# One base row on GpSimd, first weights loaded a stage ahead, and identity products on TensorE in a macaron block (mixture of experts, attention, mixture of experts)

## The reference

```python
x = x + 0.5 * ffn(layernorm(x), w_router, w_gate, w_up, w_down)
x = x + attn(layernorm(x), Wq, bq, Wk, bk, Wv, bv, Wo, bo)     # 16 heads of 32, RoPE, softmax
x = x + 0.5 * ffn(layernorm(x), w_router, w_gate, w_up, w_down)

# ffn: xt is [8192, 512], 32 experts, capacity C = 320 rows per expert
logits = xt @ w_router
top1 = argmax(softmax(logits)); gate = the probability of top1
pos = cumsum(onehot(top1))[t, top1] - 1; accepted = pos < C
slot = top1 * C + pos                       # rows over the capacity are dropped
y = (silu(buf @ w_gate) * (buf @ w_up)) @ w_down   # per expert
return xt + where(accepted, y[slot] * gate, 0)
```

## Time and profile before

| | |
|---|---|
| median of three runs | 4290.29 us |
| the profiled execution's own time | 4291.16 us |
| its span in the trace | 4289.4 us |
| mean granted TensorE clock | 0.962 of 2.4 GHz |
| PE, PEld, DVE, ACT, POOL busy | 94%, 61%, 69%, 49%, 57% |
| r1 | 0 to 212 us |
| e1 | 212 to 970 us |
| qkv | 970 to 1577 us |
| attention | 1577 to 3239 us |
| r2 | 3239 to 3532 us |
| e2 | 3532 us to the end |

### The profile page before, as it was taken

The page is one execution under the profiler, slowest core; times in us unless marked ns, Lnnn a source line. Parts: engine busy times, 40 slices in busy tenths (PEclk is TensorE's granted clock), DMA queues, the critical chain, the costliest instruction groups (busy, mean ns, idle before and its releaser), DMA issues. The chain is left out here.

```text
span 4289.4 us, 68901 instructions
## 1 busy us (share of the span) xinstructions
PE 4027.0 (94%) x24768; PEld 2627.7 (61%) x24768; DVE 2957.0 (69%) x3993; ACT 2106.5 (49%) x3591; POOL 2434.7 (57%) x1500
## 2 busy tenths in 40 slices
PE   5489999998999979999999999999996969999999
PEld 3379899886888853333333333333335758998998
DVE  5567777766666667777777777777744866777776
ACT  5433333332222217777777777777772434333332
POOL 2334334324555647888888888888881333443442
PEclk7589999998999989999999999999998989999999
DMA  6265555535555555656665666656636845555552
GB/s 220 99 213 197 171 184 194 175 120 185 182 175 182 177 150 131 134 132 137 139 141 130 135 138 143 134 130 137 140 87 224 290 156 203 196 188 174 187 193 105
DMA packets 493061, 700.29 MB, mean 163 GB/s; under 512 B 217684, under 2 KB 220008, under 8 KB 492752
## 3 DMA queue, kind: packets, MB, share of 16 engines
q1 hardware_dynamic: 459984, 629.09, 52.0%
q0 software_dynamic: 30720, 66.62, 4.1%
q10 hardware_dynamic: 2048, 0.53, 0.1%
HBM read 518.55 MB, written 194.54 MB: 166 GB/s over the span
## 5 line engine op out<-in xcount | busy, mean ns | idle before, releaser
L1858 DVE TENSOR_REDUCE kept_big<-att_mx 128x2 f32<-128x2048 f32 x496 | 1137.5, 2293 | 436.4 <-PE att_mx L1892 436.1
L1802 ACT ACTIVATE att_p<-att_st 128x512 f32<-128x512 f32 x2048 | 1086.8, 602 | 412.6 <-PE att_st L1915 350.8
L1762 POOL TENSOR_TENSOR att_pairsum<-att_p,att_p 128x1024 f32<-128x1024 f32 x512 | 1207.2, 2383 | 87.8 <-ACT att_p L1802 74.1
L944 ACT ACTIVATE e_sg<-e_gp 128x320 f32<-128x320 f32 x256 | 112.1, 438 | 732.7 <-PE e_up L208 684.1
L925 DVE TENSOR_TENSOR e_w<-e_raw,e_w 128x2048 fp32r<-128x2048 f32 x192 | 439.1, 2287 | 41.9 <-ACT e_w L920 40.8
L1915 PE MATMUL att_st<-att_q,att_k 128*128 128x512 f32 x1344 | 452.6, 438 | 0.2 <-ACT att_p L1802 0.2
L1915 PEld LDWEIGHTS att_st<-att_q,att_k 128*128 128x128 f32 x1344 | 216.1, 187 | 327.2 <-ACT att_p L1802 220.0
L920 ACT ACTIVATE e_w<-e_raw 128x2048 fp32r<-128x2048 f32 x192 | 367.0, 1911 | 53.1 <-DMA e_raw<-in_w_gate 49.1
L1925 PE MATMUL att_st<-att_p,att_v 128*32 128x512 f32 x2688 | 349.3, 603 | 0.0
L389 POOL DMA_INDIRECT table<-r_pay,r_slot_i x128 | 143.4, 1121 | 354.8 <-DVE r_pay L577 320.7
L894 POOL DMA_INDIRECT x<-e_xg,e_meta x64 | 102.3, 1599 | 410.4 <-DVE e_xg L987 388.4
(11 more groups left out here) (177 smaller groups left out, 8262.2 us busy)
## 6 DMA issues: line engine op xcount, KB each, us to landing
e_raw<-in_w_gate SPq DMA_DIRECT2D x64, 1024.0 KB
e_raw<-in_w_up SPq DMA_DIRECT2D x64, 1024.0 KB
e_raw<-in_w_down SPq DMA_DIRECT2D x64, 1024.0 KB
r_ao<-ao SPq DMA_DIRECT2D x32, 1024.0 KB
att_q<-q SPq DMA_DIRECT2D x126, 256.0 KB, 5.3
att_k<-k SPq DMA_DIRECT2D x126, 256.0 KB, 7.4
kept_w<-q SPq DMA_DIRECT2D x110, 256.0 KB, 4.7
kept_w<-k SPq DMA_DIRECT2D x66, 256.0 KB, 7.3
```

Of the source, the lines that this page charges most:

```text
L1762: nc.gpsimd.tensor_tensor(out=pairsum[h][g][:, :], in0=pr[h][2 * g][:, :], in1=pr[h][2 * g + 1][:, :], op=ALU.add).then_inc(s_add, 1)
L1802: nc.scalar.activation(pr[h][kt][:, half(c)], st[u % NB], ACT.Exp, scale=SCALE).then_inc(s_exp, 1)
L1858: nc.vector.tensor_reduce(out=big[p % 2][:, :, qt], in_=mx[:, :, :, :].rearrange("p h c k -> p h (c k)"), axis=AX.X, op=ALU.max).then_inc( ...
```

## The change

It has three parts.

First, in r1 alone, the base row of the last tile of each group (j = 3) is made by POOL instead of ACT, with a multiply and an add by the same two vectors. ACT makes three (`OURS`). The waits on `s_base` count three, and a new semaphore `s_side` counts POOL's.

Second, weights go a stage ahead. Two tiles of 1 MB are kept over two stages. In a routing stage SP loads gate and up of expert 0 into them when group 13's base has been stored; in e1, behind the last expert's loads, SP loads wq and wv into the same two tiles once expert 30's weights are split. In qkv ACT makes the high parts of wq and wv before the first `norm`, and DVE the low part of wq before it measures the first group.

Third, `keep_busy` gives PE plain float32 products of the 128x128 identity with itself, whose result nobody reads. In r1 three of them stand in front of every turn from group 1 on and of every `products` from group 2 on; 36 stand at the end of r1 and r2, 28 at the start of e1 and e2, 20 at the start of qkv, 40 at the end of attention.

```diff
+def keep_busy(nc, out, ident, n):
+    for _ in range(n):
+        nc.tensor.matmul(out[:, 0:P], ident[:, :], ident[:, :], start=True, stop=True)
 # route, sync
             def store_base(r):
-                sp.wait_ge(s_base, TJ * (r + 1))
+                sp.wait_ge(s_base, OURS * (r + 1))
+                if not attn:
+                    sp.wait_ge(s_side, r + 1)
...
                 store_base(r)
+                if r == NG - 3:
+                    for tile, src, landed in first:
+                        sp.dma_start(tile[:, :, :], src).then_inc(landed, 16)
 # route, gpsimd
+            def last_base(r):
+                j = TJ - 1
+                pool.wait_ge(s_lin, 2 * (r + 1))
+                pool.wait_ge(s_base_stored[r % 2], 16 * (r // 2))
+                nc.gpsimd.tensor_scalar(base[r % 2][:, j, :], x[r % NX][:, j, :], grow[r % 2][:, j:j + 1],
+                                        shift[r % 2][:, j:j + 1], ALU.mult, ALU.add).then_inc(s_side, 1)
...
             for w in range(NR):
+                if not attn and w + 1 < NR:
+                    last_base(2 * w + 2)
                 pool.wait_ge(s_slots, w + 1)
                 for j in range(TR):
+                    if not attn and w + 1 < NR and j == TR // 2:
+                        last_base(2 * w + 3)
                     nc.gpsimd.indirect_dma_start(
 # route, scalar (three places)
-                        bases(r, range(TJ))
+                        bases(r, range(OURS))
 # route, tensor
                     if r < NG:
                         for j in range(TJ):
+                            keep_busy(nc, spare, ident, 3)
                             turn(r, j)
                     positions(w)
                     if r < NG:
+                        keep_busy(nc, spare, ident, 3)
                         products(r)
                         for j in range(TJ):
+                            keep_busy(nc, spare, ident, 3)
                             turn(r + 1, j)
+                        keep_busy(nc, spare, ident, 3)
                         products(r + 1)
...
+            keep_busy(nc, spare, ident, 36)
 # experts
             load_meta(0, 0)
-            load_raw(0, 0, (0,))
             sp.dma_start(ident[:, :], cst["ident"]).then_inc(s_const, 16)
-            load_raw(0, 0, (1,))
...
+            for w, (src, landed) in enumerate(after):
+                sp.wait_ge(s_hi, 3 * (E - 2) + w + 1)
+                sp.wait_ge(s_lo, 3 * (E - 2) + w + 1)
+                sp.dma_start(raw[w][0][:, :, :], src).then_inc(landed, 16)
...
+            keep_busy(nc, yp[0], ident, 28)
             for m in range(KH):
                 turn(0, 0, m)
 # qkv, scalar
+            hi_w(ORDER[0])
+            hi_w(ORDER[1])
             norm(0, 0)
-            hi_w(ORDER[0])
 # qkv, vector
+            lo_w(ORDER[0])
             measure(0, 0, (0, 1))
             measure(0, 0, (2, 3))
             normalise(0, 0)
-            lo_w(ORDER[0])
+            lo_w(ORDER[1])
 # qkv, tensor
+            keep_busy(nc, pps[:, 0, :], ident, 20)
 # attention, tensor, at its end
+            keep_busy(nc, mx[:, 0, 0, :], ident, 40)
```

More of the change, by code:

```diff
@@ L223, in route @@
     NA = 3
+    OURS = TJ if attn else TJ - 1
     with S.ctx:
@@ L467, in _ @@
                     if r < NG:
-                        bases(r + 1, range(TJ))
+                        bases(r + 1, range(OURS))
         @block.vector
@@ L739, in _, with experts @@
                         back(r + 1)
-def experts(nc, name, moved, rows, table, wg, wu, wd, cst):
+            keep_busy(nc, spare, ident, 36)
+def experts(nc, name, moved, rows, table, wg, wu, wd, cst, first, after=()):
     S = Space(nc, name)
@@ L755, in experts @@
         side = sb("side", [P, 1])
-        raw = [S.pair(sb, f"raw{w}", [P, KD, F]) for w in range(3)]
+        raw = [[tile, sb(f"raw{w}", [P, KD, F])] for w, (tile, _, _) in enumerate(first)]
+        raw.append(S.pair(sb, "raw2", [P, KD, F]))
         split = [[S.pair(sb, f"w{w}_{par}", [P, KD, F], F32R) for par in range(2)] for w in range(3)]
@@ L915, in hi_weight @@
             e, par = number(i, b), b % 2
-            act.wait_ge(s_raw[w][par], 16 * (turns(i, b) + 1))
+            if w < 2 and par == 0:
+                act.wait_ge(first[w][2], 16)
+                act.wait_ge(s_raw[w][par], 16 * turns(i, b))
+            else:
+                act.wait_ge(s_raw[w][par], 16 * (turns(i, b) + 1))
             act.wait_ge(s_gu, past(KF * (e - 1)))
@@ L1108, in _, with qkv @@
             rounds_out(DEPTH, E, step)
-def qkv(nc, name, x_in, wT, bias, cst, q_out, k_out, v_out, kept):
+def qkv(nc, name, x_in, wT, bias, cst, q_out, k_out, v_out, early_w, kept):
     S = Space(nc, name)
@@ L1127, in qkv @@
         w = [S.pair(sb, f"w{m}", [P, KD, D], F32R) for m in range(3)]
-        area = [sb(f"area{m}", [P, 4, GROUP]) for m in range(3)]
+        area = [early_w[m][0] if m in early_w else sb(f"area{m}", [P, KD, D]) for m in range(3)]
         wraw = area
@@ L1990, in macaron, with early @@
              for n, many in (("r1", 2), ("e1", 8), ("r2", 2), ("e2", 8))}
-    route(nc, "r1", moved["r1"], x, w_router, cst, x1, table[0])
-    experts(nc, "e1", moved["e1"], x1, table[0], w_gate, w_up, w_down, cst)
-    with Kept(nc) as kept:
-        qkv(nc, "qkv", x1, (wq, wk, wv), (bq, bk, bv), cst, q, k, v, kept)
-        attention(nc, "att", q.rearrange("s b d q -> s (b d) q"), k.rearrange("s b d q -> s (b d) q"),
-                  v.rearrange("b g t c -> (b g) t c"), cst, ao.rearrange("s b d q -> s (b d) q"), sums, inverse, kept)
-    route(nc, "r2", moved["r2"], x1, w_router, cst, out, table[1], attn=(ao, wo, bo))
-    experts(nc, "e2", moved["e2"], out, table[1], w_gate, w_up, w_down, cst)
+    def early(kept, name):
+        tiles_of = [kept.enter_context(nc.sbuf_tensor(f"{name}_first{w}", [P, KD, F], F32)) for w in range(2)]
+        return [(tile, src[0:1, :, :].rearrange("o (k p) f -> p (o k) f", p=P),
+                 nc.alloc_semaphore(name=f"{name}_first_in{w}"))
+                for w, (tile, src) in enumerate(zip(tiles_of, (w_gate, w_up)))]
+    with ExitStack() as kept:
+        first = early(kept, "e1")
+        landed = [nc.alloc_semaphore(name=f"w_landed{m}") for m in range(2)]
+        after = [(src.rearrange("(k p) n -> p k n", p=P), sem) for src, sem in zip((wq, wv), landed)]
+        early_w = {m: (first[w][0], landed[w]) for w, m in enumerate((0, 2))}
+        route(nc, "r1", moved["r1"], x, w_router, cst, x1, table[0], first)
+        experts(nc, "e1", moved["e1"], x1, table[0], w_gate, w_up, w_down, cst, first, after)
+        with Kept(nc) as held:
+            qkv(nc, "qkv", x1, (wq, wk, wv), (bq, bk, bv), cst, q, k, v, early_w, held)
+            attention(nc, "att", q.rearrange("s b d q -> s (b d) q"), k.rearrange("s b d q -> s (b d) q"),
+                      v.rearrange("b g t c -> (b g) t c"), cst, ao.rearrange("s b d q -> s (b d) q"), sums, inverse, held)
+    with ExitStack() as kept:
+        first = early(kept, "e2")
+        route(nc, "r2", moved["r2"], x1, w_router, cst, out, table[1], first, attn=(ao, wo, bo))
+        experts(nc, "e2", moved["e2"], out, table[1], w_gate, w_up, w_down, cst, first)
 def constants(np):
```

32 lines of the change are left out of this document (22 added, 10 removed).

## The result

The changed kernel takes 4276.4 us (median of 7 runs) where the kernel before takes 4290.3, a ratio of 0.9968 with the interval 0.9958 to 0.9977. The profiled execution took 4276.7 us with a span of 4274.9, 14.5 less than before. By the first instruction of each stage, r1 gave 11.0 of them (e1 begins at 201.4 in place of 212.4), e1 1.3, qkv 0.8, e2 1.7, and attention with r2 took back 0.3.

The account below looks back on a forecast made before the run. PE is nearly full elsewhere; only r1, a chain with no engine full, and the seams, some 350 of 4289 us, were reachable. Terms -16 (r1), -9 (e1, e2), -1 (qkv), 0 gave -26: 4264 us, range 4243 to 4286.

Parts of the forecast that it names:

- Part 1: r1, base row on POOL at 1.2 us: -0.7 us a round in the second half, up to +1.2 in the first.
- rival (a): r1: held-back events vanish as turns come earlier in the scatters; rounds of 17.5 us, 4244 us in all; chance 0.16.
- Part 2: r1, identity products: clock up for most of r1, both products 1.08 us; rounds of 20.7 us, r1's term -16 us.
- the second half's sum: r1, second half of a round: base row 0.7, products 1.7 and last turns 0.2 make it 2.6 us shorter.
- the 0 for the first half: r1, first half of a round: scatters' +1.2 against faster positions and shorter ACT; 0 us, between -3 and +1.3.
- rival (b): Only the seams pay: scatters set r1's first half, DVE's chain eats the rest; r1 0, sum -10, 4280 us; chance 0.12.
- Part 3: e1 and e2: gather 2.9 us sooner, gate and up at full clock; some -4.5 us each, -9 for both.
- qkv: Start of qkv: projecting begins later, at 990.6, but at full clock; -1 us in all, bounds +2.3 and -3.
- Attention to r2: Seam into r2: 0 us, as PE still waits for a DMA after 40 products and nothing warms it.
- Rival (c): r1: clock stays at half, rounds of 28 us; +33 less 10 at the seams, 4313 us; chance 0.06.
- rival (d): Seams: gather late by its own latency, cold products delay turns; e1, e2 +1.5 each, qkv +2; 4279 us; chance 0.08.

Follow-up runs that it names:

- best: Changed kernel with products only in r1's second halves and e1/e2 starts (seven more there), second base row behind the scatters, qkv's low parts earlier: 4265.7 us, 0.9951 of before.
- base_act: Changed kernel with all four base rows on ACT again, all identity products kept: 4289.8 us, 1.0006 of the kernel before.
- no_products: Changed kernel without any identity product; weights ahead and the base row on GpSimd stay: 4267.2 us, 0.9955 of the kernel before.
- no_seam: Changed kernel with the threes in r1's rounds but without the 36, 28, 20 and 40 products at stage ends and starts: 4275.3 us, 0.9972 of before.
- late_again: Changed kernel with identity products only in the second half of r1's rounds, none at the seams, on chip D: 4267.8 us, 0.9956 of before.
- after_again: The changed kernel, unchanged, run again on chip D: 4274.7 us, 0.9972 of the kernel before.
- orders_np: Changed kernel without products, DVE's low parts moved ahead at the starts of e1, e2 and qkv: 4236.6 us, 0.9974 of before on chip C.

## Why the prediction was right or wrong

The time was in the range and on the right side, at half the forecast's gain (14.5 of 26 us). Every stage gave less than its term: r1 11.0 for 16, e1 and e2 3.0 for 9, qkv 0.8 for 1. And in r1 even the sign of a term was wrong: one part gave far more than its price and the other took instead of giving. That their sum came to 11 of 16, and the time into the range, is luck.

**Part 1** put the base row on GpSimd at -0.7 us a round, and at up to +1.2 in the first half. The price was too high (0.78 us, not 1.2), and its effect was mis-sized most: -2.3 a round and -16.0 in r1 on chip B. I had counted ACT's time in the second half only. ACT is free earlier in the first half too, and the turns' events come 4.5 us earlier; that they come before the scatters hold anything back is the likely reason, not shown by itself. The next event is still late, so 1.1 us a round is left of it. That is rival (a)'s mechanism, in part. It came with the base row and, it seems, not by the pause: best, on D and with products in the second half, has no pause, and its turns come through as early. On C, where nothing is held back, the weights and the base row together are worth only 3 us.

**Part 2** had the second half's sum: 13.8 to 11.4 us is -2.4 for -2.6, at PEclk 0.85. But it had it by luck. I let both products fall to 1.08 us; the first ones stayed at 1.86 to 1.94 in four of the six rounds, as PE stands before them, and 0.6 came from where I had nothing, the second products' event, no longer late.

The step that failed is the 0 for the first half. Up to the products it measured +1.1 (copies at 9.9 for 8.9 us), inside my bound, and the 1.2 of the base row, rival (b), isn't the whole of it: base_act has no base row among the scatters, and its last copies come 10.9 us after choose. What the term should have been is read from the last scatter. On A, B and D ACT's copy behind the first products starts after the end of the last scatter in 58 of 60 rounds; on C, with eight scatters, it starts 1.4 to 5.1 us before that end in all 18. So where events are late the scatters close the first half, and a faster PE only brings choose nearer to them. In the changed kernel the last scatter ends 10.4 us after choose and that copy follows 2.1 us later; in no_products these are 9.5 and 0.9. Of the 2.1 us in all, 0.9 is choose coming earlier against the scatters and 1.2 is PE's work coming later behind them.

The net is a median 8.0 us longer with the threes, from no_products to no_seam on B; the threes of the first half alone cost 6.8 from late_again to after_again on D, with the small part of the seams in it. On C the clock that the products raise is worth 14 us.

The Trainium skill (TensorE: Matmul & The Clock Gate, Part 4) says that transposes don't count as busy time of PE in the same way. With 0.59 without products and 0.85 with them the runs on B and A agree; on C orders_np rose to 0.76 with no product, so transposes and routing products alone don't always leave it at half.

**Part 3.** The gather came 1.9 us sooner, not 2.9. The clock at the first turn is full, as forecast, but it fell behind PE's 2.33 us between the turns, and gate and up ran at half: the 2.4 of the matmuls' clock were not gained. That made -1.3 and -1.7 of -4.5 each. no_seam and no_products show that the 28 products gave nothing that the stages' times can tell: what is left is the weights. best, with seven products in that place, keeps the clock at 1.0, but of the 2.4 a stage no more than 1.3 shows in its stages' times, for a reason that stays open.

**qkv** was -0.8 for -1, projecting later than before as forecast (19.5 us after the begin, 20.5 forecast). That it came near is two errors again: projecting began 1.0 us sooner than forecast, and its first 5.7 us ran at half the clock where I had it full. That the low part ahead of the statistics could not use the time before was a choice of the kernel and no necessity: the wait for the identity can stand behind it.

**Attention to r2** gave nothing, as said; r2's first matmul is at half the clock. Rival (c) is wrong, the clock rose; rival (d) is wrong in the gather and in the turns. Rival (b), only the seams pay, is wrong too: r1 gave 11.0. But its ground, a first half closed by the scatters, is what the runs bear out.

**Open.** What holds PE's events, and in best its issue, during the scatters on A, B and D and not on C. The traces show that it isn't the scatters alone, since C has them too, nor anything in the kernel, since one kernel ran both ways. That more instructions on PE make it worse is shown in part, by the 1.2 us above. Whether it belongs to a chip or to the time of a run can't be told, as each chip was used at one time only. How the number of scatters bears on it was not tested where events are late.

## What to carry to other kernels

Filling an engine's gaps to keep its clock up can cost more than it gives where other work depends on its events being prompt. Price each part of a change with a run of its own: the whole (0.9968) hid that it is 0.9955 without the products. Measure a wait from the event that ends it, here the last scatter, and not from the start of the round, which moves when something else gets faster. A clock gained at a seam is kept only if the gaps behind it are filled too, down to the first dense matmuls. And a gain that hangs on late events is to be measured on more than one chip before it is believed. Stage times are of one execution; look how far it lies from its kernel's median before reading a few us out of them.

## What was unexpected of the hardware

One kernel took 4287.5 us on one chip and 4248.7 on another, with no such wait of ACT in the traces of four other kernels on the second, and 17 to 39 us of it in 40 to 190 us in the traces of the other chips. GpSimd's multiply and add of 128x512 with two scalars a row takes 0.78 us where its sum of two such tensors takes 1.30. 56 matmul instructions of the identity took 7.93 us in e1, 0.14 each, with the clock rising in them. An indirect DMA of the gather takes 1.00 us to issue on GpSimd beside an idle DVE, and 1.87 beside DVE's subtraction of 128x2048.
